# Tile 0's neighbour products twelve steps behind the products with W, its chunk transposes at steps 10, 18, 26 and 31

## The reference, cut to what matters

```python
deg = jnp.maximum((adj != 0).astype(jnp.float32).sum(-1), 1.0)
# graph layer on xn = layernorm(x)
a_hat = adjacency + jnp.eye(n, dtype=adjacency.dtype)
dinv = jax.lax.rsqrt(node_degree)
pooled = (dinv * a_hat * dinv) @ xn + xn
x = x + jax.nn.relu(pooled @ W + b)
# then x = x + ffn(layernorm(x)), top 2 of 16 experts
```

## Time and profile before

| | |
|---|---|
| median of 3 runs | 635.46 us |
| lowest and highest run | 632.73 and 636.9 us |
| the profiled execution | 633.52 us |
| its span, first to last instruction | 632.0 us |
| granted clock, mean of the span | 0.981 |
| PE busy | 585.1 us (93%) |
| DVE busy | 462.2 us (73%) |
| ACT, POOL busy | 237.2 us (38%), 308.9 us (49%) |

### The profile page before, as it was taken

One profiled execution on the slowest core, in us unless ns is written; L12 is line 12 of the kernel. 1 busy time (PEld: TensorE's weight loads), 2 busy tenths in 40 slices (PEclk: granted clock), 3 DMA queues, 4 the chain that ended last, 5 costly groups with the idle time before them and its releaser, 6 DMA issues. The chain is left out here.

```text
span 632.0 us, 17051 instructions
## 1 busy us (share of the span) xinstructions
PE 585.1 (93%) x4756; PEld 461.9 (73%) x4757; DVE 462.2 (73%) x1469; ACT 237.2 (38%) x483; POOL 308.9 (49%) x361
## 2 busy tenths in 40 slices
PE   7899999999999999999748998999899999999993
PEld 6687888888888888888616665766666767676772
DVE  5777899999999999999746776666655555655661
ACT  3563344434444334344314444444332323233331
POOL 7333466666666666663352233443343444434443
PEclk9999999999999999999959999999999999999997
DMA  8966999999999999996567536676444444444420
GB/s 222 220 119 154 191 204 213 209 213 213 214 211 210 208 215 209 205 220 199 181 197 263 115 83 136 148 169 148 73 71 75 80 69 71 68 76 69 75 40 1
DMA packets 67596, 95.73 MB, mean 151 GB/s; under 512 B 9312, under 2 KB 42112, under 8 KB 67040
## 3 DMA queue, kind: packets, MB, share of 16 engines
q0 software_dynamic: 33408, 52.42, 47.6%
q1 hardware_dynamic: 32672, 40.88, 21.8%
q10 hardware_dynamic: 1472, 1.88, 0.9%
HBM read 103.71 MB, written 26.94 MB: 207 GB/s over the span
## 5 line engine op out<-in xcount | busy, mean ns | idle before, releaser
L502 PE MATMUL bank<-wall,at_xg 128*128 128x257 f16 x1024 | 238.7, 273 | 4.9 <-DVE at_xg L877 4.5
L504 PE MATMUL bank<-wall,at_xg 128*128 128x256 f16 x1024 | 233.6, 273 | 0.0
L1363 POOL DMA_INDIRECT out_dram<-orows,at_xg x79 | 122.8, 1554 | 170.2 <-DMA out_dram<-orows,at_xg 134.3
L624 PE MATMUL bank<-wall,feat 128*128 (+1 forms) x474 | 117.7, 385 | 11.7 <-issue 9.3
L804 ACT ACTIVATE hgs<-hgs 128x512 f32<-128x512 f32 x79 | 49.8, 630 | 195.1 <-DVE hgs L1181 195.1
L1187 DVE SCALAR_TENSOR_TENSOR hl<-bank,xseT 128x512 f16<-128x512 f32 x79 | 54.7, 692 | 92.2 <-ACT xseT L810 92.2
L502 PEld LDWEIGHTS bank<-wall,at_xg 128*128 128x128 f16 x1024 | 102.9, 100 | 21.6 <-DVE at_xg L877 8.3
L1331 POOL DMA_INDIRECT rows<-feat,posi x64 | 73.4, 1146 | 86.9 <-issue 84.5
L504 PEld LDWEIGHTS bank<-wall,at_xg 128*128 128x128 f16 x1024 | 100.3, 98 | 15.4 <-DVE wall L884 0.3
L650 PE MATMUL bank<-wall,xseT 128*128 (+1 forms) x632 | 108.0, 273 | 0.0
L624 PEld LDWEIGHTS bank<-wall,feat 128*128 128x128 f16 x474 | 46.0, 98 | 61.0 <-issue 27.4
(11 more groups left out here) (152 smaller groups left out, 764.9 us busy)
## 6 DMA issues: line engine op xcount, KB each, us to landing
abuf<-in_adj_dram POOLq DMA_DIRECT2D x128, 256.0 KB, 6.5
wst<-in_L_ffn_W_dram SPq DMA_DIRECT2D x32, 512.0 KB, 11.3
at_xg<-rows SPq DMA_DIRECT2D x79, 136.0 KB, 2.4
out_dram<-orows SPq DMA_DIRECT2D x32, 128.0 KB
abuf<-in_L_ffn_b_dram SPq DMA_DIRECT2D x4, 1024.0 KB, 8.2
wall<-in_x_dram SPq DMA_DIRECT2D x10, 256.0 KB, 13.3
rows<-pad POOLq DMA_DIRECT2D x11, 136.0 KB, 6.2
out_dram<-orows,at_xg POOLq DMA_INDIRECT x79, 3.8
```

What stands on the lines that cost most here:

```text
L502: both = [lambda: pe.matmul(ps_acc[odd][:, 0:D + 1], w, yh[:, j, 0:D + 1], start=j == 0, stop=j == T - 1), lambda: pe.matmul(ps_acc[odd][: ...
L504: lambda: pe.matmul(ps_acc[odd][:, 0:D], w, yl[:, j, :], start=False, stop=False)]
L624: mm = pe.matmul(q_h[r % 2][:, :], a, w, start=n == 0, stop=n == 3 * DC - 1)
L1363: L.indirect_dma_start(out, bass.IndirectOffsetOnAxis(ap=info[r][:, 0:1].bitcast(U32), axis=0), orow[r], None, bounds_check=N - 1, oob_is_ ...
```

## The change

`LAG` goes from 6 to 12. TensorE's neighbour products of tile 0 begin in step 12 and not 6, the first part has 44 steps and not 38, and the last 12 hold neighbour products only. VectorE transposes tile 0's chunks in steps 10, 18, 26 and 31; before, it was steps 4, 10, 18 and 26. The own edges are added in step 10. Nothing else differs: the same instructions run, with the same operands.

```diff
--- before.py
+++ after.py
@@ -49,7 +49,8 @@
 JC = CW // P
 AB = 4
 DEPTH = 2
-LAG = 6
+LAG = 12
+TURNS = (10, 18, 26, 31)
 GROUPS = ((0, 2), (2, 5), (5, 8)) + tuple((n, n + 4) for n in range(8, 32, 4))
 LEAD = 6
 SG = 2.0 ** 8
@@ -897,10 +898,10 @@
             low_y(n)
             if n + LEAD < T:
                 stats_up_to(n + LEAD)
-            if n in (XT // 2, XT + 2, 2 * XT + 2, 3 * XT + 2):
-                if n < XT:
+            if n in TURNS:
+                if n == TURNS[0]:
                     add_own(0, 0)
-                transpose_chunk(0, 0, n // XT)
+                transpose_chunk(0, 0, TURNS.index(n))
             if n == T // 4 + 2:
                 after(V, "gb_high", 0)
                 V.scalar_tensor_tensor(out=gbm[P // 2:P, :], in0=gb[P // 2:P, :], scalar=SG, in1=gbm[P // 2:P, :],
```

## The result

The changed kernel takes 644.55 us, median of 6 runs (641.04 to 649.99); the kernel before took 635.98 in the same comparison (6 runs, 632.73 to 636.99). The ratio is 1.0148, with a 95% interval of 1.0116 to 1.018. The forecast was 637.5 and a range up to 641.0: the loss is three times the one that was worked out.

A forecast was written before the change was run, and what follows sets the result against it. TensorE was taken to bound the adjacency stage. A later start of tile 1 (+1.6 us) and a tile 2 wait for the late weight part (+1.2) gave +2.8 on the 634.65 average: 637.5 us, range 634.0 to 641.0.

The forecast's parts named there:

- The bound: Adjacency stage goes at TensorE's pace once tile 1 has begun; any move of that start carries to the stage's end.
- the fifth: Before tile 1's first neighbour product: its first chunk comes behind one more transpose, a TensorE wait of 0.2 us.
- check of +1.6 by waits: Start of tile 1 later by +1.6 us, cross-checked by TensorE's waits: 4.7 us before, 6.5 after.
- First wait: TensorE's wait for chunk 0 in tile 0: 3.4 us in place of 3.0, a loss of 0.4.
- rival four: Clock falls in the 3.4 us wait for chunk 0: 640.5 us, or 643 with a second fall; chance 0.08.
- The rule that was weighed: TensorE clock: recurring gaps can each bring half rate, and transposes don't count as work; the forecast didn't use it.
- What hangs on chunk 3: Later adjacency loads of tile 4 delay the first FFN weight part; TensorE waits 1.2 us in tile 2, bounds 0 and 1.7.
- 1.7 to 1.9 delays the weight part: Of 2.8 us of moved adjacency transfer, 1.1 at most finds room; the rest delays the first FFN weight part, to 64.4.
- Rival three: TensorE's waits for transposed adjacency really go, winning their 4.5 us: 631.0 us to the median; chance 0.05.

The follow-up runs named there:

- both: Changed kernel with chunk 0's transpose ahead of the stats that wait for x, and the first FFN weight part loaded directly behind x: 633.59 us, ratio 0.9953.
- w_ahead_of_pads: Changed kernel with SyncE's two big transfers behind b2 swapped, the first FFN weight part issued ahead of the pad rows: 637.65 us, ratio 1.0007.
- dose30: Changed kernel with tile 0's chunk transposes at steps 6, 14, 22 and 30, lag still twelve: 637.59 us, ratio 1.0027.
- filled: Changed kernel with 30 products of constants, result unused, put on TensorE before its wait for chunk 0: 643.51 us, ratio 1.0121.
- w_early: Changed kernel with only the first FFN weight part's load moved directly behind the x loads on SyncE's queue: 636.73 us, ratio 1.0016.
- before_w: Kernel before the change with only the first FFN weight part loaded early, behind the last x load: 636.58 us, ratio 0.9999.
- turn_first: Changed kernel with only step 10 reordered: own edges and chunk 0's transpose ahead of the stats that wait for x: 641.52 us, ratio 1.0074.
- spread: Changed kernel with tile 0's chunk transposes at steps 6, 14, 22 and 26, lag still twelve: 630.08 us, ratio 0.9905.

## Why the prediction was wrong

**What held.** The bound: a later start of tile 1 was carried to the end. Four waits instead of two appeared ahead of tile 1, where they were placed; the fifth, of 0.2 before tile 1, didn't come. Tile 1 was to start 1.4 us earlier by the neighbour products put off, and later by the chunk waits; `both` shows this sum right to 0.2 us, in part by luck: its waits for chunks 1 to 3 were each 0.2 shorter than worked out and the last was missing, so some 0.7 us of other time in that stretch made up for them. The prediction's check of +1.6 by waits was loose too: it took 1.7 for the wait of 1.56, and 6.5 less the 4.5 of the earlier trace rows is 2.0. That VectorE would wait for the x piece was right (2.36 us, 1.6 forecast), and so were both places of loss: the x piece ahead of chunk 0, and the weight part behind tile 4's adjacency.

**First wait, the landing of x.** The step "landed 15.6 us later, at 24.8" took one execution's landing for a fixed time. In the changed kernel's profile it was 25.8, and VectorE's waits for it ended at 25.17 in `w_ahead_of_pads`, 25.72 in `both` and 24.21 in `dose30`; in `filled` the load had landed at 22.3. Chunk 0 was used at 27.27, 1.0 later than the 26.3 that was worked out.

**The clock.** It was left out of the sum and given to rival four with 0.08. The prediction itself had put the wait at 3.4, above the longest with full clock, and said that it decides there. Of the waits for chunk 0 those of 3.54, 4.10 and 4.12 us brought 0.50, one of 2.96 and shorter ones did not. But 3.0 is no threshold: idle times of 1.91 and 1.93 us near the start brought 0.50 in `w_early` and `before_w`. The fall cost 2.7 us in the first part, against 3 forecast by the rival, whose 6 us at the lower level no row of before had shown; they were about 6 here. With its second fall, the rival's 643 is the nearest to what came. The rule that was weighed, in the Trainium skill (TensorE: Matmul & The Clock Gate, HAM oscillation — how this bites in real kernels), is borne out in part: the gaps of 4.12 and 6.37 us were each followed by 0.50, the one of 2.96 before the change was not. The other one (Part 4: PE-mode transpose) doesn't show: from 16 to 23 us, with f32 transposes and W products alone, the clock of the changed kernel was 1.00. As W products stood between the transposes, that is no test of transposes by themselves.

**What hangs on chunk 3.** This is the step that failed most. "1.7 to 1.9 delays the weight part" counted only the 2.8 us of two moved transfers. The prediction named the pad rows ahead of it on the same queue, but gave their lateness no term, and a delay that grows on the way none either. The runs show the first: the pad rows took 10.4 us and not 5.5, and with the weight part put ahead of them (`w_ahead_of_pads`) it landed after 7.7. The lateness was 7.3 us (13.5 against 6.2), not 1.9; TensorE's wait 6.37, not 1.2. The clock fell in that wait too: tile 2's own product to tile 3's took 87.19 - 70.79 = 16.40 us where it had been 73.74 - 65.64 = 8.10, so 8.3 lost, of which 6.4 is the wait; for the other 1.9 the clock at 0.50 behind it is the likely reason.

**The sum in the profiled execution:** 5.2 + 8.3 = 13.5 of the 13.6 us. This is the account of one long execution against one short one, and not of the 8.6 between the medians. On medians, by the experiments: the weight part 7.8 (`w_early`), the x wait with its clock 3.0 (`turn_first`), and the two together 11.0 (`both`). What is left after both is 3.2 below the kernel before.

**Rival three** ended on the side that it named for other settings of the same idea: with all transposes early enough and chunk 0 before the wait for x (`spread`), the lag of twelve wins 6.8 us on the medians. That is more than the 4.5 which the prediction called the most, since those were the waits of a single, short execution.

Not settled is how the DMA engines divide their time between the two queues. The Trainium skill (DMA: Bandwidth & Descriptors, Queues, rings and completion order) says that each engine takes turns between the queues that have work, a packet at a time. The rows agree in kind: with tile 4's first quarters issued 3.8 us or more ahead of them, the pad rows took 5.5 us or less, with 0.7 to 1.2 us 8.8 to 10.9. How large a packet is, and what a load that casts costs against one that doesn't, wasn't measured. Nor was the clock's part in tile 2 measured by itself, nor what besides the length of a gap decides whether the clock falls.

## What to carry to other kernels

A step that frees a buffer sets when the next loads are issued; before it is moved, look which transfer was alone in the DMA engines until then, what stands ahead of it on its own queue, and what will be issued while it is late. Place a transpose by two sides: before the next operation on its engine that waits for a load, and several steps before its use. A landing time in one profile is a sample; a chain that hangs on it needs a margin of a microsecond or more, and an idle gap near the longest one that kept full clock must be costed with the clock. A shorter gap isn't safe by its length alone.

## What the runs showed of the hardware

With tile 4's first quarters issued 1.2 us ahead and not 5.0, the pad rows took 8.8 us to land where they had taken 5.5, and the 512 KB load behind them 12.9 where it had taken 6.2: here the delay grew along the queue. And a wait can cost more than it lasts. Behind an idle time of 3.54 us ahead of chunk 0 TensorE needed 34.31 - 32.76 = 1.55 us more for the same work, behind 4.12 us 2.7 more, since it ran at 0.50 from inside the wait until about 33 us; behind 1.72 us and less it needed nothing more. The length of an idle time doesn't settle this alone: 2.96 us in the kernel before left the clock at 1.00, while 1.91 and 1.93 us near the start of two other executions were followed by 0.50.
